# A state-space layer with a gated feed-forward on one core: the product into the state in three rounded products

## What is computed

```python
zxbcdt = hidden_states @ in_proj_w.T                 # gate, x, B, C, dt
xBC = silu(conv(xBC) + conv_b)                       # 4 taps along the tokens
dt = softplus(dt + dt_bias); A = -exp(A_log); xs = x * dt
L = exp(segment_sum(A * dt))
Gm = einsum('bcihn,bcjhn->bhcij', C, B)
Y_diag = einsum('bhcij,bcjhd->bcihd', Gm * L, xs)
states = einsum('bckhn,bhck,bckhd->bchdn', B, decay_states, xs)   # the product into the state
Y_off = einsum('bckhn,bchdn,bhck->bckhd', C, states_before, state_decay)
y = (Y_diag + Y_off + D * x) * silu(gate)
var = mean(y * y, over the group)                    # groups of 1024 channels
out = (y * rsqrt(var + EPS) * norm_w) @ out_proj_w.T
```

## Time and profile before

| | |
|---|---|
| median of 3 runs | 1938.36 us |
| the profiled execution | 1938.42 us, its span 1936.7 us |
| mean granted TensorE clock | 0.994 |
| PE busy | 1885.4 us, 97% of the span |
| DVE, ACT, POOL busy | 1455.2, 1169.8, 953.1 us |
| product into the state (line 1098) | 224 records, 107.4 us busy |
| sum of squares (line 1655) | 64 operations, 129.2 us busy |

### The profile page before, as it was taken

How to read it: one execution, slowest core, us unless ns; L and a number is a source line. 1 busy time by engine, 2 the same in 40 slices (tenths; PEclk the granted TensorE clock), 3 DMA queues, 4 the chain that set the end, 5 groups by cost and what they waited for, 6 DMA issues and landing times.

```text
span 1936.7 us, 29309 instructions
## 1 busy us (share of the span) xinstructions
PE 1885.4 (97%) x10416; PEld 1477.4 (76%) x10416; DVE 1455.2 (75%) x1701; ACT 1169.8 (60%) x1908; POOL 953.1 (49%) x693
## 2 busy tenths in 40 slices
PE   6998999999999999999999999999999999999997
PEld 4776777777777777777777777878787878787875
DVE  6876746878787877778786878686878787877776
ACT  3334346767677676767676556566665656565643
POOL 6656643555555455555454444444344444444333
PEclk9999999999999999999999999999999999999998
DMA  2324463445454646464646253433424242525231
GB/s 88 120 79 145 135 217 98 135 164 182 147 191 136 210 131 227 131 210 129 210 129 234 86 167 116 120 108 98 141 77 156 83 161 83 156 73 155 69 124 44
DMA packets 123102, 264.62 MB, mean 137 GB/s; under 512 B 18112, under 2 KB 24384, under 8 KB 122704
## 3 DMA queue, kind: packets, MB, share of 16 engines
q1 hardware_dynamic: 88240, 161.55, 26.4%
q10 hardware_dynamic: 34720, 101.20, 16.5%
HBM read 216.82 MB, written 45.88 MB: 136 GB/s over the span
## 4 chain that ended last, share of the span: by engine, by line
PE 87%; DMA 3%; POOL 3%; DVE 2%; issue 2%; ACT 2%; ACTq 0%; SPq 0%; DVEq 0%; POOLq 0%
PE bank L1065 39%; PE bank L1123 6%; PE bank L1164 6%; PE bank L1185 6%; PE bank L1178 5%; PE bank L1098 5%; PE bank L1085 5%; PE bank L1130 3%; PE bank L721 3%; PE bank L694 3%; PE bank L1110 3%; PE bank L680 1%; POOL wxp L314 1%; DMA wosl<-wlo_scratch 1%; PE bank L1154 1%
## 5 line engine op out<-in xcount | busy, mean ns | idle before, releaser
L1065 PE MATMUL bank<-xnp,wxp 128*128 128x512 f32 x3432 | 863.3, 404 | 7.9 <-POOL wxp L1444 3.1
L1065 PEld LDWEIGHTS bank<-xnp,wxp 128*128 128x128 f32 x3432 | 635.5, 189 | 160.0 <-POOL wxp L1444 11.0
L1444 POOL TENSOR_TENSOR wxp<-wxs,wxp 128x512 fp32r<-128x512 f32 x286 | 382.2, 1339 | 535.2 <-ACT wxp L1294 534.7
L1544 DVE SCALAR_TENSOR_TENSOR conv<-bank,cws,conv 128x509 f32<-128x509 f32 (+2 forms) x480 | 358.1, 746 | 11.3
L1301 ACT ACTIVATE conv<-bank,cbs,cws 128x512 f32<-128x512 f32 x160 | 124.3, 777 | 281.2 <-PE bank L1065 266.1
L1475 POOL TENSOR_TENSOR yl<-gT,yh 128x1024 fp32r<-128x1024 f32 x63 | 152.1, 2415 | 210.1 <-ACT yh L1359 210.1
L1294 ACT ACTIVATE wxp<-wxs 128x512 fp32r<-128x512 f32 x286 | 178.1, 623 | 0.1
L1647 DVE SCALAR_TENSOR_TENSOR M<-M,gb 128x1024 f32<-128x1024 f32 x128 | 172.5, 1349 | 7.5 <-DVE gb L1639 0.5
L1345 ACT ACTIVATE ya<-xT,dch 128x128 f32<-128x128 f32 x512 | 156.2, 392 | 0.0
L1336 ACT ACTIVATE M<-bank 128x1024 f32<-128x1024 f32 x64 | 65.7, 1026 | 136.8 <-PE bank L1130 136.8
L1178 PE MATMUL bank<-wosh,yh 128*128 128x512 f32 x512 | 136.7, 409 | 5.0 <-issue 5.0
(11 more groups left out here) (166 smaller groups left out, 2850.2 us busy)
## 6 DMA issues: line engine op xcount, KB each, us to landing
wxs<-wp SPq DMA_DIRECT2D x288, 256.0 KB, 2.7
wosh<-whi_scratch ACTq DMA_DIRECT2D x64, 512.0 KB, 6.2
wosl<-wlo_scratch ACTq DMA_DIRECT2D x64, 512.0 KB, 11.6
ecs<-ecs_scratch ACTq DMA_DIRECT2D x112, 256.0 KB, 4.5
stage<-wout SPq DMA_DIRECT2D x64, 256.0 KB, 3.0
whi_scratch<-stagh SPq DMA_DIRECT2D x64, 256.0 KB, 2.0
wlo_scratch<-stage SPq DMA_DIRECT2D x64, 256.0 KB, 2.3
wxs<-w SPq DMA_DIRECT2D x56, 256.0 KB, 2.8
```

The lines of the kernel that those rows point to most:

```text
L1065: last = pe.matmul(bank(k), wxp[:, k % 2, a, kk, :], xnp[:, b, kk, :], start=kk == 0 and a + b == 0, stop=kk == KT - 1 and a == 1)
L1444: pool.tensor_tensor(wxp[:, k % 2, 1], wxs[:, k % AHEAD], wxp[:, k % 2, 0], ALU.subtract).then_inc(w_lo, 1)
L1544: last = dve.scalar_tensor_tensor(out=conv[:, n % CB, back:], in0=bank(k)[:, 0:TH - back], scalar=cws[:, g, j, i:i + 1], in1=conv[:, n % C ...
```

## The change

The product into the state is made from split operands: `xdec` into `xdech` (ACT, `high_x`) and `xdecl` (POOL, `low_x`), the keys `gb[:, 1]` into `gbh` (ACT, `high_b`) and `gbl` (POOL, `low_b`); PE makes three rounded products for each of the two halves. The low parts lie in the same memory as the full values, which they overwrite (`twice`). The low part of the gated output, `yl` before, is now written over the gated output itself (`gTl`), so `low_y` waits for the square. `ys` is gone too: the sums go into the first 128 places of the squares, and the squares are laid out with the 8 tiles of a token side by side.

```diff
+    def twice(name, shape):
+        with ExitStack() as once:
+            full = sb(once, name, shape)
+        return full, sb(ctx, name + "l", shape, F32R)
-        gT = [sb(ctx, f"gT{p}", [P, XT, TH]) for p in range(2)]
+        gT, gTl = zip(*(twice(f"gT{p}", [P, XT, TH]) for p in range(2)))
-        xdec = sb(ctx, "xdec", [P, GC])
+        xdec, xdecl = twice("xdec", [P, GC])
+        xdech = sb(ctx, "xdech", [P, GC], F32R)
-        yl = sb(ctx, "yl", [P, XT, P], F32R)
-        ys = sb(ctx, "ys", [P, P])
-        gb = sb(ctx, "gb", [P, 2, P])
+        gb, gbl = twice("gb", [P, 2, P])
+        gbh = sb(ctx, "gbh", [P, P], F32R)
...
         def squares(q):
-            return xdt[:, q % 2].rearrange("p (t i) -> p t i", t=XT)
+            return xdt[:, q % 2].rearrange("p (i t) -> p t i", t=XT)
+        def square_sums(q):
+            return xdt[:, q % 2, 0:P]
+        def gated_low(q):
+            return gTl[q // CH % 2][:, :, tokens(q)]
...
             def into_state(q):
-                pe.wait_ge(x_dec, done(q + 1))
-                pe.wait_ge(g_cp, done(q + 1))
+                pe.wait_ge(x_lo, done(q + 1))
+                pe.wait_ge(b_lo, done(q + 1))
                 pe.wait_ge(e_b, done(q + 1))
                 for b in range(2):
-                    last = pe.matmul(X[:, b * 512:(b + 1) * 512], gb[:, 1, :], xdec[:, b * 512:(b + 1) * 512],
-                                     start=True, stop=True)
+                    part = slice(b * 512, (b + 1) * 512)
+                    pe.matmul(X[:, part], gbh[:], xdech[:, part], start=True, stop=False)
+                    pe.matmul(X[:, part], gbh[:], xdecl[:, part], start=False, stop=False)
+                    last = pe.matmul(X[:, part], gbl[:, 1], xdech[:, part], start=False, stop=True)
                 last.then_inc(st_mm, 1)
...
+            def high_x(q):
...
+                act.wait_ge(x_dec, done(q + 1))
+                act.activation(xdech[:], xdec[:], ACT.Copy).then_inc(x_hi, 1)
+            def high_b(q):
...
+                act.wait_ge(g_cp, done(q + 1))
+                act.activation(gbh[:], gb[:, 1], ACT.Copy).then_inc(b_hi, 1)
             act.wait_ge(left, 1)
...
+                if k == 15:
+                    high_x(0)
+            high_b(0)
             skip(0)
             load_ecs(1)
...
                 if q and more:
                     load_ecs(q + 1)
+                if more:
+                    high_x(q + 1)
                 if fill:
                     load_low(q // CH)
...
                 square(q)
                 if more:
                     exp_b(q + 1)
+                    high_b(q + 1)
                 load_row(q + 2)
...
             def low_y(q):
                 u, _, _, _ = place(q)
-                pool.wait_ge(o_mm, done(q))
+                pool.wait_ge(y_sq, done(q + 1))
                 if q + 1 < CELLS:
                     pool.wait_ge(y_hi, done(q + 1))
-                    pool.tensor_tensor(yl[:], gT[u % 2][:, :, tokens(q)], yh[:], ALU.subtract).then_inc(y_lo, 1)
+                    pool.tensor_tensor(gated_low(q), gT[u % 2][:, :, tokens(q)], yh[:], ALU.subtract).then_inc(y_lo, 1)
...
+            def low_x(q):
...
+                pool.wait_ge(x_hi, done(q + 1))
+                pool.tensor_tensor(xdecl[:], xdec[:], xdech[:], ALU.subtract).then_inc(x_lo, 1)
+            def low_b(q):
...
+                pool.wait_ge(b_hi, done(q + 1))
+                pool.tensor_tensor(gbl[:, 1], gb[:, 1], gbh[:], ALU.subtract).then_inc(b_lo, 1)
...
             for k in range(TILES):
                 low(k + 2)
+                if k == 15:
+                    low_x(0)
+            low_b(0)
             join(0)
             for q in range(CELLS):
                 two = slices(q)
-                for k in tiles_of(q)[:2]:
+                for k in tiles_of(q)[:1]:
+                    low(k + 2)
+                if q + 1 < CELLS:
+                    low_x(q + 1)
+                for k in tiles_of(q)[1:2]:
                     low(k + 2)
...
                 low_y(q)
+                if q + 1 < CELLS:
+                    low_b(q + 1)
...
             def sum_tiles(q):
                 dve.wait_ge(y_sq, done(q + 1))
                 dve.wait_ge(q_mm, done(q))
-                dve.tensor_reduce(ys[:], squares(q).rearrange("p t i -> p i t"), AX.X, ALU.add).then_inc(y_s, 1)
+                dve.tensor_reduce(square_sums(q), squares(q).rearrange("p t i -> p i t"), AX.X, ALU.add).then_inc(y_s, 1)
```

More of the change, by code:

```diff
@@ L873, in scan @@
         y_rn, skip_d = sem("y_rn"), sem("skip_d")
+        x_hi, x_lo, b_hi, b_lo = sem("x_hi"), sem("x_lo"), sem("b_hi"), sem("b_lo")
         halo_step, halo_d = sem("halo_step"), sem("halo_d")
@@ L1184, in project_out @@
                 for t in range(XT):
-                    last = pe.matmul(y_out, yl[:, t, :], wosh[:, t, :],
+                    last = pe.matmul(y_out, gated_low(q)[:, t, :], wosh[:, t, :],
                                      start=False, stop=c > 0 and t == XT - 1)
@@ L1193, in square_sum @@
                 pe.wait_ge(y_s, done(q + 1))
-                pe.matmul(Y[:, 2 * P:2 * P + 1], ys[:], one[:], start=True, stop=True).then_inc(q_mm, 1)
+                pe.matmul(Y[:, 2 * P:2 * P + 1], square_sums(q), one[:], start=True, stop=True).then_inc(q_mm, 1)
             for k in range(TILES):
@@ L1241, in scalar @@
         def scalar(act):
-            for s in (tap_d, silu_d, z_d, e_a, e_b, y_sq, y_hi, skip_d):
+            for s in (tap_d, silu_d, z_d, e_a, e_b, y_sq, y_hi, skip_d, x_hi, b_hi):
                 act.sem_inc(s, CREDIT)
@@ L1364, in high_y @@
                         act.activation(yh[:, part], gT[u % 2][:, part, tokens(q)], ACT.Copy).then_inc(y_hi, 1)
+            def high_x(q):
+                if dead(q):
+                    act.sem_inc(x_hi, 1)
+                    return
+                act.wait_ge(x_dec, done(q + 1))
+                act.activation(xdech[:], xdec[:], ACT.Copy).then_inc(x_hi, 1)
+            def high_b(q):
+                if dead(q):
+                    act.sem_inc(b_hi, 1)
+                    return
+                act.wait_ge(g_cp, done(q + 1))
+                act.activation(gbh[:], gb[:, 1], ACT.Copy).then_inc(b_hi, 1)
             act.wait_ge(left, 1)
@@ L1437, in gpsimd @@
             pool.wait_ge(d_const, 16 * 5)
-            for s in (u2_d, y_lo, y_rn, halo_step, halo_d):
+            for s in (u2_d, y_lo, y_rn, halo_step, halo_d, x_lo, b_lo):
                 pool.sem_inc(s, CREDIT)
@@ L1479, in low_y @@
                         pool.wait_ge(y_hi, done(q + 1 + n))
-                        pool.tensor_tensor(yl[:, part], gT[u % 2][:, part, tokens(q)], yh[:, part],
+                        pool.tensor_tensor(gated_low(q)[:, part], gT[u % 2][:, part, tokens(q)], yh[:, part],
                                            ALU.subtract).then_inc(y_lo, 1)
+            def low_x(q):
+                if dead(q):
+                    pool.sem_inc(x_lo, 1)
+                    return
+                pool.wait_ge(x_hi, done(q + 1))
+                pool.tensor_tensor(xdecl[:], xdec[:], xdech[:], ALU.subtract).then_inc(x_lo, 1)
+            def low_b(q):
+                if dead(q):
+                    pool.sem_inc(b_lo, 1)
+                    return
+                pool.wait_ge(b_hi, done(q + 1))
+                pool.tensor_tensor(gbl[:, 1], gb[:, 1], gbh[:], ALU.subtract).then_inc(b_lo, 1)
             def rest_of(n):
```

## The result

The changed kernel takes 1962.25 us (median of 4 runs, 1959.89 to 1967.19) against 1937.87 us for the kernel before on the same chip: a ratio of 1.0123, 95% interval 1.0108 to 1.0138. It is slower by 24 us; the prediction had 1934.2, with 1942 as its upper end. The profiled execution took 1959.89 us and spans 1958.1.

A forecast was written before the change was run, and what follows sets the result against it. The prediction took TensorE (PE) to bound the kernel inside the scan. From 1938.4 us, -17.4 + 3.4 + 3.9 + 5.3 + 0.6 = -4.2 gave 1934.2 us, slower rival C outside the range of 1925 to 1942.

The forecast's parts named there:

- Part 4: New layout of the squares: ACT's strided write takes 1.85 us, PE waits 0.43 us for `yl` in 9 units, +3.9 us.
- Part 1: Product into the state: six rounded products take 1.41 us instead of 1.72, in 56 cells, -17.4 us.
- Part 2, the start: First product into the state, cell 0: waits for the splits until 321.5 instead of 318.68, once +3.4 us.
- Part 2, `high_x` at c = 0: ACT at c = 0: `high_x` moves the `wosl` transfers, second tile's tap, convolution, gating, `yh` and square back 1.0 us.
- Part 3: `low_y` overwrites the gated output and waits for the square: covered, with 0.37 us to spare at c = 0.
- Part 5: Units 2 to 6, c = 0 and 1: held by transfers, savings swallowed; with 0.2 for unit 1, +5.3 us.
- Part 6: The tail, last 52 us: shorter sums against the DVE-POOL lock, net 0 (-3 to +3); +0.6 us for lost saving.
- C: Rival at `project_out`, c = 0: POOL loses the lock to DVE's weighing of M, 2.8 us per unit, 1969 us; chance 0.09.
- A: Rival on the squares' layout: the strided write is free, Part 4 is 0, 1930.3 us; chance 0.27.
- B: Rival on splits and transfers: splits hide fully, transfers do not bind, only the start is paid, 1924.4 us; chance 0.08.
- D: Rival across all cells: waits of 0.3 us eat the slots, nothing measurable, 1936 to 1941 us; chance 0.18.

The follow-up runs named there:

- e1: The changed kernel with the squares written in one run again and the sums put into a dead slice of the queries: 1941.31 us, ratio 1.0013.
- e5: e1 with the product into the state of cell 0 left whole in fp32 and unsplit: 1931.05 us, ratio 0.9986.
- e11: e7 with the squares laid out in pairs (step of 8 bytes): 1927.59 us, ratio 0.9941.
- e3: The changed kernel with the plain fp32 product into the state, no splits, and the squares in one run: 1936.17 us, ratio 0.999.
- e7: e5 with the product into the state whole in fp32 in cells 60 and 61 too: 1929.46 us, ratio 0.9974.
- e14: e11 without the splits of `xdec` (`high_x`, `low_x`) in units 1 to 7, PE's work the same: 1930.92 us, ratio 0.9957.
- e15: e14 with the keys not split in units 1 to 7 either, PE's work the same: 1923.55 us, ratio 0.9918.
- e8: e3 with the squares laid out in pairs (ACT writes with a step of 8 bytes): 1926.37 us in a single run.
- e12: The kernel of e8, timed (no splits, squares in pairs): 1934.09 us, ratio 0.9982.
- e2: The changed kernel with the plain fp32 product into the state and no splits, the strided squares kept: 1947.17 us, ratio 1.0043.

## Why the prediction was wrong, step by step

The step that failed is Part 4, which let the longer square count at `yl` alone, in nine units, +3.9 us. After against e1 measured it at 20.9. The other parts together came nearer: 17.4 us of slots saved, 5.5 lost at the start and 13.0 in units 1 to 7 make +1.1, and e1, which has all of these and not the strided square, measured 2.5 us above before.

**Part 1** was right. The chain of after, behind the square sum, where the earlier trace rows had 1.82:

```profile
349.89 0.34 PE bank L1114
350.23 0.23 PE bank L1115
350.46 0.23 PE bank L1116
350.69 0.23 PE bank L1114
350.93 0.23 PE bank L1115
351.16 0.24 PE bank L1116
351.39 0.87 PE bank L1127 x8
```

These are 1.50 us, 0.32 less, and in units 8 to 14, where nothing else changed, the split kernels take 6.9 us less than the unsplit ones (713.9 to 707.0) for 20 products: 0.34 each.

**Part 2, the start**, was too small: 3.4 us predicted, 5.5 on average in the profiled executions (6.5 between the two spans), 5.2 from e1 to e5. Two terms failed. After's timeline of POOL (its first two lines) and PE, then the stretches, of which before had a clock of 1.00 in both:

```profile
319.79 2.02 POOL L1481 TENSOR_TENSOR wxp<-wxs,wxp 128x512 fp32r<-128x512 f32 x1 [0.76 <-ACT wxp L1311]
321.77 1.43 POOL L1532 TENSOR_TENSOR gbl<-gb,gbh 128x128 fp32r<-128x128 f32 x1
...
323.30 0.76 PE L1114 MATMUL bank<-xdech,gbh 128*128 128x512 f32 x1 [4.42 <-issue]
```

```profile
317.00:323.00 6.00, 1.89 (x10) 1.38 (x8) 3.86 (x3) 3.65 (x11) 5.24 (x4) 0.84 0.24 74
323.00:328.00 5.00, 4.70 (x15) 4.04 (x16) 1.28 (x2) 0.00 (x0) 0.20 (x1) 0.51 0.75 215
```

`low_b` took 1.43 us instead of 0.5, while DVE's two weighings of M ran, and ended at 323.2 instead of 321.5; 0.8 us of this is that all of it came later (gb at 318.93, 318.15 before). And PE, idle for 4.4 us, came back at a granted clock of 0.51, so at 1.2 GHz: the product took 2.9 us instead of 1.4 and the transposes 1.71 instead of 0.87, another 2.3 us which my sum didn't have.

**Part 2, `high_x` at c = 0**: 1.0 us was charged for ACT, and the rounding overlaps the issues (e11's first two lines above). In units 8 to 14 of the kernel before, the second tile's tap started 0.7 to 1.2 us behind the diagonal at c = 0, and so it does in e11. What does come late by 0.5 us is `yh`. DVE's small addition, held by `low_x` (0.81 us above instead of 0.16), lies on its way and is as late. So the effect had half my size and another cause.

**Part 3** was right: by e3 the wait for the square costs nothing where the square takes 1.05 us.

**Part 4** is the step on which the prediction fell. The price of the write was mis-sized, 1.85 against 2.23 us, but that is 0.4 us. (DVE's strided pace, which I took as its bound, is 2.02 us and not 1.9.) The larger error is where I let it count: at `yl` alone, in nine units, 3.9 us. At c = 0 of the second half this was near: 24.9 us in after and 24.3 in e1, 4.2 us for the seven (I had 3.0). But the whole costs 21 us. Units 1 to 7 have 11.9 of it (741.3 - 729.4), of which I had counted units 1 and 7 at 0.43 each and left out the others as "held by transfers": 8.8 at c = 0, 3.3 at c = 1. At c = 0 of these units PE waits 7.3 us for `yl` (1.2 in e1). So a unit in which PE waits for transfers at one place was not covered against a late `low_y` at another. ACT's waits for the `stage` slices did not grow in these units (20.5 us in after, 21.3 in e1), so that the transfers themselves were held back by the square isn't shown. Units 8 to 14 have 6.7, the 4.2 and 2.7 at c = 3, which I hadn't looked at. From cell 60 on it is 3.2, within this column's spread, though PE's waits for the low part there rose from 1.1 to 3.6 us.

**Part 5** had the right place, and half the size or less. With squares that cost nothing the units lose 9.3 us of slots in e11 (725.7 - (725.1 - 8.7)) and up to 13.6 in e7, and I had 5.3. I had priced the keys' split at 0.4 us a unit; the medians of e14 and e15 differ by 1 us for each of the seven units.

**Part 6**: from cell 60 on nothing changed (67.2, 67.4), as said. The parts behind it aren't resolved: this column spreads by 3.7 us between two profiled executions of one kernel (e8 and e12), and the granted clock differs there too.

**The rivals.** C named a mechanism that came in three of the sixteen c = 0 cells: in units 3, 5 and 15 `low_y` was lengthened to 3.43, 2.74 and 3.04 us, and PE waited 1.6, 1.9 and 2.9. In unit 3 it was the scaling of S that got ahead, by 10 ns with a square of 2.22 us, and not the weighing that C had named behind one of over 3. The other waits come from the later start alone (2.4 us for `low_y` as before). A, B and D were further off. What was missing was the case in which two delays, each of them covered or nearly so, exceed the cover together.

## What to carry to other kernels

Cover is spent once. Two delays on the way to the same wait can each cost little and much more together, so add up the delays first and compare the sum with the cover, at every wait behind them. Neither "covered" nor "in full" is a rule for a stretch where the bound engine already waits for others: here the same longer square cost units 1 to 7 3.7 us without the splits (e2 - e3) and 11.9 with them (each good to some 4 us), while leaving out 1.06 us on ScalarE and 2.4 on GpSimd in every cell of these units gained nothing (e14). Such a stretch wants a run with each piece left out, and one with both. Price a layout on the writer as well as on the reader, and try pairs before going from one extreme to the other. Look at what stands beside a GpSimd operation: between convolutions it took 2.4 us, among VectorE's large operations 3.1 on average, with up to 1.8 more on one of VectorE's.

## What was not expected of the hardware

- ACT's writes of fp32 elements cost 1.05, 1.12, 2.05 and 2.23 us per 128x1024 at steps of 4, 8, 16 and 32 bytes.
- ACT computed while transfers that stand behind the computation in its own queue were issued (1255.36 and 1255.38 above), but not the other way round (1266.45 behind 1264.32 + 2.09).
- A VectorE operation on three elements took 0.81 and 1.78 us instead of 0.16 while GpSimd subtracted, and a 128x128 subtraction on GpSimd 1.30 on average, 0.44 at its shortest: measured against its own length, the lock cost the small operation most.
- After 4.4 us without work PE ran at a granted clock of 0.51, which is 1.2 GHz, in the stretch 323 to 328 us. The start of cell 0 moved by up to 7 us between executions of kernels with the same code ahead of it, the later ones at a mean granted clock of 0.98 over the first 325 us and the earliest at 1.00.
